# TensorE's attention program written out for all 256 steps instead of two written-out passes around a loop

## What is computed

```python
def _L0_xattn_ref(query, context, w_q, w_kv, w_out, b_out):
    q = query @ w_q
    kv = context @ w_kv
    k, v = jnp.split(kv, 2, axis=-1)
    q = q.reshape(B, NQ, NUM_HEADS, HEAD_DIM).transpose(0, 2, 1, 3)
    k = k.reshape(B, NKV, NUM_HEADS, HEAD_DIM).transpose(0, 2, 1, 3)
    v = v.reshape(B, NKV, NUM_HEADS, HEAD_DIM).transpose(0, 2, 1, 3)
    scores = jnp.einsum('bhqd,bhkd->bhqk', q, k) * SCALE
    attn = jax.nn.softmax(scores, axis=-1)
    out = jnp.einsum('bhqk,bhkd->bhqd', attn, v)
    out = out.transpose(0, 2, 1, 3).reshape(B, NQ, INNER)
    return out @ w_out + b_out
...
x = x + _L0_xattn_ref(_layernorm(x, axis=-1), ctx_768, ...)      # x: 32 x 64 x 256, context: 32 x 1601 x 192
x = x + _L0_attn_ref(_layernorm(x, axis=-1), ...)
x = x + _L0_ffn_ref(_layernorm(x, axis=-1), ...)
```

## Time and profile before

| | us |
|---|---|
| median of 3 runs | 2573.53 |
| lowest and highest | 2570.07, 2574.76 |
| profiled execution, its own time | 2574.86 |
| its span, first to last instruction | 2573.1 |
| from the span's start to 200 (queries, and the first steps) | 200 |
| 200 to 2092 (attention) | 1892 |
| 2092 to the end (output, recurrence, feed-forward) | 481 |

### The profile page before, as it was taken

The page is one execution under the profiler, slowest core; times in us unless marked ns, Lnnn a source line. Parts: engine busy times, 40 slices in busy tenths (PEclk is TensorE's granted clock), DMA queues, the critical chain, the costliest instruction groups (busy, mean ns, idle before and its releaser), DMA issues. The chain is left out here.

```text
span 2573.1 us, 43052 instructions
## 1 busy us (share of the span) xinstructions
PE 2355.1 (92%) x13872; PEld 2145.3 (83%) x13872; DVE 1710.9 (66%) x2666; ACT 1516.0 (59%) x2459; POOL 1700.7 (66%) x873
## 2 busy tenths in 40 slices
PE   4969999999999999999999999999999947855777
PEld 3649999999999999999999999999999945744666
DVE  7766666666666666666666666666666626768762
ACT  4646666666666666666666666666666525543342
POOL 2007788888888888888888888888888632023452
PEclk9989999999999999999999999999999968986888
DMA  5957878888788888888777788878888549910000
GB/s 158 259 155 190 193 193 198 194 192 193 194 192 195 199 194 195 197 198 197 192 193 195 192 193 200 196 192 199 196 198 195 131 102 219 187 50 0 9 9 17
DMA packets 387378, 434.18 MB, mean 169 GB/s; under 512 B 45652, under 2 KB 362232, under 8 KB 387320
## 3 DMA queue, kind: packets, MB, share of 16 engines
q1 hardware_dynamic: 387320, 433.45, 69.2%
HBM read 162.73 MB, written 52.43 MB: 84 GB/s over the span
## 5 line engine op out<-in xcount | busy, mean ns | idle before, releaser
L550 POOL TENSOR_TENSOR p_pt_lo<-p_landed,p_pt_hi 128x768 fp32r<-128x768 f32 (+1 forms) x512 | 1005.1, 1985 | 359.9 <-ACT p_pt_hi L614 359.9
L789 PE MATMUL p_acc<-p_nat,p_pt_hi 128*128 128x384 f32 x3328 | 978.5, 362 | 14.1 <-POOL p_pt_lo L550 13.8
L791 PE MATMUL p_acc<-p_nat,p_pt_lo 128*128 128x192 f32 x3328 | 845.7, 254 | 0.0
L646 ACT ACTIVATE p_prob<-p_scores,p_negmax 128x800 f32<-128x800 f32 (+1 forms) x512 | 471.2, 926 | 515.7 <-DVE p_negmax L719 515.7
L773 PE MATMUL p_scores<-p_ct_hi,p_q_hi 128*128 128x512 f32 (+2 forms) x2048 | 710.2, 350 | 24.2 <-DVE p_ct_hi L746 13.8
L773 PE MATMUL p_scores<-p_ct_hi,p_q_lo 128*128 128x512 f32 (+2 forms) x2048 | 705.1, 348 | 0.0
L725 DVE STREAM_TRANSPOSE turned<-p_prob 128x1664 f32<-128x1664 f32 x256 | 489.5, 1912 | 317.0 <-ACT p_prob L646 317.0
L789 PEld LDWEIGHTS p_acc<-p_nat,p_pt_hi 128*128 128x128 f32 x3328 | 630.7, 190 | 16.5 <-issue 13.7
L791 PEld LDWEIGHTS p_acc<-p_nat,p_pt_lo 128*128 128x128 f32 x3328 | 640.8, 193 | 0.0
L614 ACT ACTIVATE p_pt_hi<-p_landed 128x768 fp32r<-128x768 f32 (+1 forms) x512 | 432.3, 892 | 159.2 <-PE p_acc L791 152.5
L773 PEld LDWEIGHTS p_scores<-p_ct_hi,p_q_hi 128*128 128x128 f32 x2048 | 388.8, 190 | 71.9 <-issue 14.3
(11 more groups left out here) (190 smaller groups left out, 2652.9 us busy)
## 6 DMA issues: line engine op xcount, KB each, us to landing
p_landed<-turned SPq DMA_DIRECT2D x2048, 104.0 KB, 2.2
shared<-in_ctx SPq DMA_DIRECT2D x96, 312.0 KB
o_scratch<-shared SPq DMA_DIRECT2D x256, 96.0 KB, 2.6
qk_scratch<-p_out_a SPq DMA_DIRECT2D x16, 1024.0 KB, 4.6
p_oa<-o_scratch SPq DMA_DIRECT2D x32, 512.0 KB, 6.0
p_stage<-qk_scratch SPq DMA_DIRECT2D x31, 512.0 KB, 3.9
p_stage<-qk_scratch SPq DMA_DIRECT2D x62, 256.0 KB, 4.2
p_stage<-in_ctxT SPq DMA_DIRECT2D x31, 401.0 KB, 3.2
```

Source lines behind the costliest of these rows:

```text
L550: nc.gpsimd.tensor_tensor(pt_lo[:, t0:t1, :, :], by_tile(slot, t0, t1), bits(pt_hi[:, t0:t1, :, :]), ALU.subtract).then_inc(pt_lo_done, 1)
L646: nc.scalar.activation(prob[:, lo:hi], scores[:, S0 + lo:S0 + hi], ACT.Exp, bias=negmax[:, par:par + 1], accum_out=rowsum[:, par, h:h + 1] ...
L789: nc.tensor.matmul(acc[k % 2][:, 0:2 * DC], pt_hi[:, t, :, :].rearrange("p i x -> p (i x)"), x[:, t, :], start=t == 0, stop=False, skip_gr ...
L791: last = nc.tensor.matmul(acc[k % 2][:, 0:DC], pt_lo[:, t, :, :].rearrange("p i x -> p (i x)"), x[:, t, 0:DC], start=False, stop=t == KT - ...
```

## The change

TensorE's call of `passes` is replaced by a plain Python loop over the 16 passes, with every pass number a constant. No matmul is added, taken away or moved, and no wait is dropped; what is compared with a register before is compared with a constant now. The other four engines keep their loops, line for line.

```diff
@@ attend_batches, block.tensor @@
             def body(r, first, last):
                 for j in range(SPP):
                     step_scores(r, j, first)
                     if not (first and j < LAG):
                         product(r, j, first)
 
-            passes(pe, body)
+            for r in range(NB // SPB):
+                body(r, r == 0, r == NB // SPB - 1)
             for j in range(LAG):
                 product(NB // SPB, j, False)
```

## The result

The changed kernel is slower: 2592.45 us (median of 6 runs, 2590.81 to 2595.16) against 2572.81 us of the kernel before on the same chips (6 runs, 2570.07 to 2574.76). The ratio is 1.0078, with a 95% interval of 1.0065 to 1.0091: 20 us. Medians and ratios are of fast executions alone; one of phase_b (2912 us) and one of the kernel before beside it on another chip (5748 us) were far slower and are left out.

A forecast was written before the change was run, and what follows sets the result against it. TensorE was taken to set the pace, busy 1881 of attention's 1892 us; removed register waits and branches gain 0, fetches that delay moves add 34 us to 2574.9, giving 2609, or 2608 for a median; range 2571 to 2635.

The forecast's parts named there:

- the likeliest case: Fetched packets make SyncE's moves late and TensorE pays, 17 to 61 us over the stage; chance 0.67.
- The removal of register waits and branches: In TensorE's loop these cost at most 0.02 us a batch, 0.6 us in all; taken as 0.
- the late moves: ScalarE would wait for `landed` in most passes, some 50 times.
- Rival (c): TensorE runs dry because packets come later than it needs them; at 1 us more each, 2685 us; chance 0.05.
- The sum: Loss over 13 loop iterations: 39.9 us if all is q8's, 27.9 by its bytes; 34 us taken.
- The phase speaks neither way: Packets slip by about 1 us a batch and pass over all places of SyncE's queue during the stage.
- a sign against itself: If passes grow but SyncE's moves still take 10.4 us, the mechanism is another one.
- Rival (a): The fetches are free, as in passes 0 and 15: added cost 0, time 2574 us; chance 0.23.
- The discount for q14: The other engines' queue also brought packets in the loop's first iteration; q8 has 70% by bytes, giving 27.9 us.
- a slack of 0.7 us: Undisturbed, a move lands at 1028.2 and ScalarE's step needing it begins at 1028.9.
- 1.0 to 1.4 us as free: A move landing that much late costs nothing; what is above that TensorE pays in full.
- The rule against it: The skill's advice to unroll: the loop fetches each iteration and pays at jumps, so the change takes 2574 us at most.

The follow-up runs named there:

- phase_b: The changed kernel with 20 idle waits a half batch in TensorE's code from batch 5 on, so a batch is exactly three packets: 2576.91 us.
- half_written_out: The changed kernel with only TensorE's passes 0 to 7 written out and passes 8 to 14 looped: 2583.29 us, ratio 1.0050 to the kernel before.
- two_pass_loop: The changed kernel with TensorE's written-out passes replaced by a register loop whose body is two passes: 2608.69 us, ratio 1.0149 to the kernel before.
- extra_packets: The kernel before, loops kept, with three plain 16 KB DMAs a batch, memory to memory, issued by ScalarE: 2571.79 us, ratio 0.9999.
- sp_written_out: The changed kernel with SyncE's program of the stage written out over constants as well: 2583.56 us, ratio 1.0051 to the kernel before.
- delay_one_move: The kernel before with two idle 8 KB DMAs issued by SyncE in the middle of one of a batch's four moves: 2600.04 us, ratio 1.0105.

## Why the prediction was right, and where it was off

**Right.** Slower was forecast, at 2608 us with a range from 2571 to 2635; it is 2592, at the lower edge of what the likeliest case alone was given (2591 to 2635). The removal of register waits and branches was costed at nothing: undisturbed batches take 59.07 us in both, and batch 14 of phase_b took 59.07 with twenty idle instructions more. The packets were foreseen at 109 and are 108; the late moves at some 50 and are 47; q8 stopping where the body stays on the chip is shown by half_written_out and two_pass_loop. Rival (c) did not happen in the written-out program: the 28 waits that no releaser is named for end with GpSimd's halves. Something like it happened at the jumps of two_pass_loop, 2.2 us each.

**Off by a term.** The sum was 13 iterations at 2.6 us (3.07 less a share for q14). From 407.34 to 1964.55 the 13 iterations took 1557.21 us against 13 x 118.19 = 1536.47: 1.6 us each. The term that was mis-sized is the loss of an iteration, taken from the only one that could be read. "The phase speaks neither way" was meant to cover this and did not: its middle packets came 28.5 and 28.9 us behind their batches' starts, where the table has its 1.1 to 1.5 us a batch; all batches of the written-out kernel lost 0.75 on average. That it was a dear sample is partly luck: in extra_packets, where TensorE's program is that of before, the same iteration and the one behind it lost 1.7 us, not 3.1. The slip of some 1 us a batch was seen, and would have told that other places come too; pass 0 and pass 15, which lost nothing, should have been taken into the mean instead of being left to a rival. Three passes with packets had lost 3.07, 0 and 0: their mean is 1.0 a pass, the measured 1.6 lies between it and 3.07.

**A second path.** The prediction let the loss come by SyncE, whose queue is held up by the length of a packet, and gave as a sign against itself that passes grow while the moves still take 10.4 us. That sign was there in part: the moves behind the seven dearest steps were issued in 10.3 to 10.4 us, and landed 1.0 to 2.2 us late. That a move lands when the slowest engine is done stood in the prediction, but had no term in the sum. These steps have 9.8 of the 22.4 us; delays that SyncE carries have a share in them (batch 8) and are the rest.

**Half right.** Rival (a) had 23%, with SyncE's written-out program in passes 0 and 15 as its reason. sp_written_out gives that a worth of some 7 us of 20. The discount for q14 moved the number the right way, and no run shows that it had a reason: 8 or 9 packets of q14 from 205 to 405 us are there in all these kernels, and nothing told their cost apart.

**The price of a late landing.** The prediction worked out a slack of 0.7 us and then put 1.0 to 1.4 us as free. The 0.7 rests on a wrong reading: the 2.2 us to landing are counted from the start of each DMA's issue, and were added to the end of the sixteenth's. The move at 1015.67 landed at 1027.7 and not at 1028.2. Measured, 1.35 us are free in step 4, and about 1.0 us of the delay in delay_one_move was. A packet of q8 took 0.9 to 1.8 us in the traces of the two kernels, where the prediction read 1.3 to 1.7 from two packets.

**The rule against it.** The section "Instruction fetch mechanics" of "Runtime: NRT & Kernel Launch" in the Trainium skill was weighed for its advice to unroll. For a body of one pass the rows spoke against it, and so did the result: unrolled, it is 20 us slower. The same section of the Trainium skill warns that a taken branch out of the window forces a fetch before work can go on. The jumps of two_pass_loop, 2.2 us each, agree with that; the jump of the one-pass loop, which costs nothing, does not.

## What to carry to other kernels

Before writing a loop out, look at the instruction queues. Here they were silent while the loop ran, its program was on the chip, and writing it out bought a packet of 16 KB every 20 us, which met whatever transfer was in the air. If TensorE's steps are equally long in a written-out pass and in a loop, there is nothing to win; look then at what fetches would meet, and how much slack the queue has that issues the next transfer. One pass with packets is one sample of their place: take the mean over all that the trace has. And look for a delay where it is paid, step by step, before a total is divided by the number of delays.

## What the runs showed of the hardware that I had not expected

A loop body of about 97 KB of TensorE's instructions was read once, in the first of 14 iterations, and not again in the other 13; one of twice that was read each time, and each jump back then left TensorE idle for 2.2 us (6 times, 13.2 us). A packet of 16 KB on the instruction queue takes 0.9 to 2.1 us over all traces. In the written-out kernel a move of 16 DMAs landed 0.7 to 2.2 us late when such a packet began within 1.1 us behind the last issue; in two_pass_loop step 4's move landed on time when it began 1.2 us behind it or later. The same bytes as 512-byte packets inside the issue cost nothing. With 108 to 110 packets in each case, their place made the loss 20, 12 or 6 us.
